# A graph-attention kernel: the two shares of a node's row weighted and added by one VectorE operation per head, with tanh in place of exp and the first three parts interleaved

## The reference

```python
N = 6250; E = 100000; IN_DIM = 256; HID = 64; HEADS = 4
h = (x @ W).reshape(n, HEADS, HID)            # x: normalised rows
e = leaky_relu(a_src[src] + a_dst[dst])       # src, dst: 206250 edges, then a self loop for each node
m = segment_max(e, dst);  num = exp(e - m[dst])
alpha = num / segment_sum(num, dst)[dst]
out = relu(segment_sum(alpha[:, :, None] * h[src], dst) + bias)
x = x + out
def step(h, _):                               # 30 times over layernorm(x)
    h = h + 0.01 * tanh(h)
    h = h * sigmoid(h)
    h = layernorm(h)
    return h @ W.T + b
x = x + (the rows after 30 steps)
```

## Time and profile before

| what | value |
|---|---|
| median of three runs | 4014.36 us (4007.2 to 4033.22) |
| the profiled execution | 4010.27 us, its span 4008.5 us |
| DVE busy | 3057.0 us (76% of the span) |
| POOL busy | 3000.3 us (75%) |
| ACT busy | 2421.6 us (60%) |
| PE busy | 1551.2 us (39%), nearly all of it after 2473 us |
| share of the chain that ended last on PE | 20%, of it the products 17% |

### The profile page before, as it was taken

One profiled execution on the slowest core, in us unless ns is written; L12 is line 12 of the kernel. 1 busy time (PEld: TensorE's weight loads), 2 busy tenths in 40 slices (PEclk: granted clock), 3 DMA queues, 4 the chain that ended last, 5 costly groups with the idle time before them and its releaser, 6 DMA issues.

```text
span 4008.5 us, 38964 instructions
## 1 busy us (share of the span) xinstructions
PE 1551.2 (39%) x7562; PEld 1329.0 (33%) x7562; DVE 3057.0 (76%) x7257; ACT 2421.6 (60%) x3681; POOL 3000.3 (75%) x2871
## 2 busy tenths in 40 slices
PE   3400000000000000000000001899999999999998
PEld 2300000000000000000000001788888888888887
DVE  7467585867768577685867766788988989888898
ACT  4334353534434344353534344689999999999997
POOL 7676676767676676766767672899999998889887
PEclk8755555555555555555555555999999999999999
DMA  7355565656555565565656563047777777777677
GB/s 201 113 177 193 182 207 181 213 174 214 195 190 201 169 223 178 190 209 168 225 164 218 189 198 126 23 117 179 189 185 185 181 177 177 173 177 175 177 183 193
DMA packets 649205, 720.45 MB, mean 180 GB/s; under 512 B 513249, under 2 KB 515458, under 8 KB 632948
## 3 DMA queue, kind: packets, MB, share of 16 engines
q1 hardware_dynamic: 563604, 486.62, 40.7%
q0 software_dynamic: 83824, 230.16, 20.0%
q10 hardware_dynamic: 1536, 1.18, 0.1%
HBM read 249.79 MB, written 352.38 MB: 150 GB/s over the span
## 4 chain that ended last, share of the span: by engine, by line
issue 25%; PE 20%; ACT 12%; DVE 12%; POOL 10%; DMA 9%; another core or an unknown queue 8%; SPq 2%; DVEq 0%; ACTq 0%; POOLq 0%
PE ps L1676 17%; ACT G L654 7%; POOL G L747 6%; DVE RS L983 5%; DMA turned<-hs 3%; DVE psum L964 3%; POOL h L1301 2%; PE ps L1662 2%; DMA h2T<-turned 2%; DMA sums<-G 2%; SPq L1231 1%; ACT hs L1398 1%; DMA G<-haug,idx 1%; ACT th L1409 1%
## 5 line engine op out<-in xcount | busy, mean ns | idle before, releaser
L747 POOL DMA_INDIRECT G<-haug,idx x1612 | 1526.6, 947 | 713.1 <-issue 481.8
L1676 PE MATMUL ps<-WT,h2T 128*128 128x256 f32 x5880 | 1338.8, 381 | 19.9 <-DMA h2T<-turned 18.8
L1676 PEld LDWEIGHTS ps<-WT,h2T 128*128 128x128 f32 x5880 | 1091.7, 191 | 175.8 <-DMA h2T<-turned 40.5
L983 DVE TENSOR_TENSOR_SCAN RS<-keep,psum 128x845 f32<-128x845 f32 x496 | 939.8, 1897 | 186.9 <-remote 109.9
L1301 POOL TENSOR_TENSOR h<-Hs,th 128x512 f32<-128x512 f32 (+1 forms) x750 | 937.8, 1262 | 129.9 <-ACT th L1409 124.6
L1068 PE MATMUL psum<-AD,ones 128*128 128x512 f32 x2 | 2.1, 1142 | 2284.9 <-DVE AD L1085 2284.9
L646 ACT ACTIVATE decay<-el,ZC 128x4 f32<-128x4 f32 x124 | 37.1, 299 | 1278.4 <-remote 568.0
L654 ACT ACTIVATE G<-RS 128x845 f32<-128x845 f32 x496 | 782.0, 1723 | 43.4 <-DVE RS L983 34.0
L1586 DVE SCALAR_TENSOR_TENSOR Hs<-ps,rs,b 128x256 f32<-128x256 f32 x1470 | 675.0, 459 | 145.3 <-PE ps L1676 132.6
L1068 PEld LDWEIGHTS psum<-AD,ones 128*128 128x128 f32 x2 | 0.5, 313 | 2285.2 <-DVE AD L1085 2285.2
L1568 DVE BATCH_NORM_STATS2 cst<-h 128x6 f32<-128x256 f32 x1470 | 546.3, 412 | 37.5 <-ACT h L1386 36.4
(11 more groups left out here) (164 smaller groups left out, 1196.9 us busy)
## 6 DMA issues: line engine op xcount, KB each, us to landing
sums<-G SPq DMA_DIRECT2D x124, 1716.0 KB
turned<-hs SPq DMA_DIRECT2D x444, 256.0 KB
G<-haug,idx POOLq DMA_INDIRECT x1612
h2T<-turned SPq DMA_TRANSPOSE x444
haug<-G SPq DMA_DIRECT2D x7, 924.0 KB
X<-x SPq DMA_DIRECT2D x7, 784.0 KB
out<-X SPq DMA_DIRECT2D x24, 224.0 KB
own<-haug SPq DMA_DIRECT2D x5, 924.0 KB, 5.5
```

Source lines behind the costliest of these rows:

```text
L747: pool.indirect_dma_start(out=G[:, u, t, :], out_offset=None, in_=haug[:, :], in_offset=bass.IndirectOffsetOnAxis(ap=idx[:, i % 2, u * T + ...
L983: v.tensor_tensor_scan(RS[:, k % 2, h, :, :].rearrange("p f t -> p (f t)"), keep[:, k % 2, :, :].rearrange("p f t -> p (f t)"), ps_m[:, h, ...
L1676: last = nc.tensor.matmul(ps_g[q.u][:, a * C:(a + 1) * C], h2T[:, q.u, (a * 2 + k) * P:(a * 2 + k + 1) * P], WT[:, k, :], start=(k == 0), ...
```

## The change

The PE products with the identity that joined the two rows go away, in all parts, with their PSUM buffers. In their place DVE's `joined` makes, for each tile and head, one scalar_tensor_tensor on 64 columns: gathered row times its weight plus the weighted own row, into `Hs`. `added` now reads this sum from `Hs` in SBUF instead of PSUM. The gathered rows' multiplication (`gathered`) goes away. The weights are made from tanh: with d = s - e, the shares 1 + tanh(d/2) and 1 + tanh(-d/2) stand in the same ratio as the two exps; the maximum is no longer taken, one operation adds the 1. ACT no longer calls exp after the attention stage; one tanh on a column is issued ahead. In parts 0 to 2 DVE's stages are interleaved (`all_spread` apart from `all_added`), ACT starts tanh after two rows instead of a whole part, POOL makes the roots of part 0 ahead of the last three fetches of part 2. The plans place a tile's join, sum and statistics at neighbouring steps; each part's rows are ready 3 or 4 steps earlier, and the table of passes shifts with it.

```diff
-PLANS = {FRONT: Plan(5, 1, 10, 17, 15, 16, 22, 23, 21, 3, 43, 48, 50, 1)}
+PLANS = {FRONT: Plan(5, 1, 10, 17, 15, 20, 18, 19, 3, 40, 45, 47, 1)}
 for b in range(FRONT + 1, NF):
     q = 24 + 80 * (b - FRONT - 1)
-    PLANS[b] = Plan(q, 8, q + 54, q + 62, q + 63, q + 64, q + 70, q + 72, q + 72, 11, q + 141, q + 148, q + 151, 3)
+    PLANS[b] = Plan(q, 8, q + 54, q + 62, q + 63, q + 69, q + 67, q + 68, 11, q + 137, q + 144, q + 147, 3)
...
             for b in range(FRONT):
                 for i in range(FT[b + 1] - FT[b]):
+                    if (b, i) == (FRONT - 1, 3):
+                        roots(0)
                     end_row(b, i)
...
-                nc.scalar.activation(share[:, b % 2, :, 0:n, :], below[:, b % 2, :, 0:n, :], ACT.Exp).then_inc(s_share, 1)
+                nc.scalar.activation(share[:, b % 2, :, 0:n, :], apart[:, b % 2, :, 0:n, :], ACT.Tanh, scale=0.5).then_inc(s_share, 1)
...
+            act.wait_ge(s_merged, 16)
+            nc.scalar.activation(spare[:, :], half_neg[:, 0:1], ACT.Tanh)
...
-                ch.add(v.tensor_tensor(nmax[:, i, 0:n, :], S[:, i, 0:n, SUMS:ROW], eself[:, t0:t1, :], ALU.max))
-                ch.wait()
-                v.tensor_tensor(below[:, i, 0, 0:n, :], S[:, i, 0:n, SUMS:ROW], nmax[:, i, 0:n, :], ALU.subtract)
-                v.tensor_tensor(below[:, i, 1, 0:n, :], eself[:, t0:t1, :], nmax[:, i, 0:n, :], ALU.subtract).then_inc(s_below, 1)
+                v.tensor_tensor(apart[:, i, 0, 0:n, :], S[:, i, 0:n, SUMS:ROW], eself[:, t0:t1, :], ALU.subtract)
+                v.tensor_tensor(apart[:, i, 1, 0:n, :], eself[:, t0:t1, :], S[:, i, 0:n, SUMS:ROW], ALU.subtract).then_inc(s_below, 1)
...
+                ch.add(v.tensor_scalar(share[:, i, :, 0:n, :], share[:, i, :, 0:n, :], 1.0, None, ALU.add))
+                ch.wait()
...
+            def joined(b, i):
+
+                for h in range(H):
+                    c = slice(h * HR, h * HR + HID)
+                    last = v.scalar_tensor_tensor(out=Hs[:, FT[b] + i, h * HID:(h + 1) * HID], in0=S[:, b % 2, i, c],
+                                                  scalar=part[:, b % 2, 0, i, h:h + 1], in1=own[:, b % 2, i, c],
+                                                  op0=ALU.mult, op1=ALU.add)
+                return last
...
-                ch.add(gathered(b, 0, n))
-                dve.wait_ge(s_own[b], 16)
-                own_rows(b, OWN_ACT[b], n).then_inc(s_scaled, 1)
+                dve.wait_ge(s_own[b % 2], 16 * (b // 2 + 1))
+                ch.add(own_rows(b, OWN_ACT[b], n))
+                ch.wait()
+                for i in range(OWN_ACT[b], n):
+                    joined(b, i)
+                dve.wait_ge(s_ownw, b + 1)
+                for i in range(OWN_ACT[b]):
+                    last = joined(b, i)
+                last.then_inc(s_scaled, 1)
...
-                if due(q, "scale"):
-                    b, i = due(q, "scale")
+                if due(q, "both"):
+                    b, i = due(q, "both")
+                    dve.wait_ge(s_joined, tiles_before(b) + i + 1)
+                    added(b, i, i + 1, Hs[:, FT[b] + i, :]).then_inc(s_taken, 1)
+                if due(q, "join"):
+                    b, i = due(q, "join")
                     if i == 0:
                         dve.wait_ge(s_part, b + 1)
-                    gathered(b, i, i + 1).then_inc(s_weighted, 1)
...
+                    dve.wait_ge(s_ownt, tiles_before(b) + i + 1)
+                    joined(b, i).then_inc(s_joined, 1)
...
-            for b in range(2):
-                shares(b)
-                norms(b)
-                all_weighted(b)
+            shares(0)
+            norms(0)
+            all_weighted(0)
+            shares(1)
             all_added(0)
+            norms(1)
+            all_spread(0)
+            all_weighted(1)
             all_added(1)
             shares(2)
+            all_spread(1)
             norms(2)
+            spread_of(At(0))
+            spread_of(At(1))
             all_weighted(2)
-            for q in range(4):
-                spread_of(At(q))
             all_added(2)
+            spread_of(At(2))
+            spread_of(At(3))
+            all_spread(2)
...
-            add_own(0)
-            add_own(1)
             transposes(At(0))
             transposes(At(1))
-            add_own(2)
...
-                if due(p, "add"):
-                    add_tile(*due(p, "add"))
```

More of the change, by code:

```diff
@@ L78, with __init__ @@
 class Plan:
-    def __init__(self, fetch, pace, below, share, norm, scale, own, add, both, step, mean, root, ready, every):
+    def __init__(self, fetch, pace, below, share, norm, own, join, both, step, mean, root, ready, every):
         n = QT
         self.at = dict(fetch=(fetch, pace, n), below=(below, 1, 1), share=(share, 1, 1), norm=(norm, 1, 1),
-                       scale=(scale, step, n), own=(own, step, n), add=(add, step, n), both=(both, step, n),
+                       own=(own, step, n), join=(join, step, n), both=(both, step, n),
                        spread=(both + 1, step, n), mean=(mean, 1, 1), root=(root, 1, 1), ready=(ready, every, n))
@@ L1180, in scan_ffn @@
         s_scaled = sem("s_scaled")
-        s_agg = sem("s_agg")
         s_added = sem("s_added")
```

90 lines of the change are left out of this document (28 added, 62 removed).

## The result

The changed kernel took 4027.45 us, the median of 12 runs (4021.8 to 4043.6), beside 4015.12 us for the kernel before, of 12 runs on the same chip (4001.63 to 4033.22). The ratio is 1.0048, with a 95% interval of 1.0031 to 1.0064 (the two medians alone stand at 1.0031): 12 to 26 us slower, where 20 us less was forecast. It lies inside the forecast range and within 1%, but on the other side of no change.

The account below looks back on a forecast made before the run. PE was taken as nearest bound, ACT right behind. Parts 4 to 7 (15), part 3 (1.5) and the front (4) sum to 20.5 us off 4010.3; with the median's 4.1 us that gives 3994 us, range 3974 to 4034.

Parts of the forecast that it names:

- PE's ceiling and ACT's loads: Parts 3 to 7: joins free PE of 30 us at most; ten ACT table loads go, 12.8 us.
- D: Rival: ACT holds the passes anyway, only 10.3 us of loads and 4 at the front count; 4000 us, chance 0.12.
- Parts 4 to 7, 15 us less: Window 2700 to 3350 us: PE loses 24.1 us, ACT 10.3, and the window shortens from 650 to 635 us.
- A head, 0.15 us: DVE's join: one operation on 64 columns takes 0.15 us, four heads of a tile 0.6 us.
- One wait for four heads, 0.5 us a tile: DVE's join: a tile's four heads go through on one wait for POOL, some 0.5 us.
- Rival A: Heads wait anew for POOL's `add`, roots let them pass; 0.8 us more per tile, 4011 us, chance 0.27.
- DVE idles 67 us, so this stays hidden: Parts 4 to 7: DVE's extra 19 us fit its idle time, busy 602 of 635 us; counted as nothing.
- Part 3, 1.5 us less: Passes 18 to 40: PE falls 0.86 us per tile, POOL does not; 1.5 us less, between 0 and 6.
- Ahead of the passes, 4 us less: Front: first tanh 5.5 us earlier, first silu only 1; 4 us less at the tanh of 2522.90, ends 1 and 5.5.
- Windows without parts that got slower, which none of this explains: Listed sign of being wrong: slower windows where no part is worked in; no size given.
- Rival B: One POOL operation between every two heads; 3.8 us more per tile, 4074 us, chance 0.09.
- C: Rival: PE's whole share comes through, ACT is no bound; 38 us less, 3976 us, chance 0.07.

Follow-up runs that it names:

- k1: Kernel before with tanh in place of exp, the maximum gone and one operation adding the 1, nothing else: ratio to before 0.9978.
- k19: The kernel of k1 again, on another chip: ratio to before 0.9994 (0.9976 to 1.0011).
- k14: Changed kernel's front and tanh, but parts 3 to 7 joined on PE with before's plans and table, part 0's roots behind the fetches: ratio to before 0.999.
- k17: k14 with parts 3 to 7 joined on DVE through PSUM instead of on PE: ratio to before 0.9968 (0.9934 to 1.0002).
- k18: The kernel of k17 again, unchanged, on the same chip as k19: ratio to before 0.9978 (0.996 to 0.9995).
- set 2: Runs on one other chip, with the kernel before and the changed kernel profiled once more: second stage 1534.2 and 1549.6 us.
- k4: Changed kernel, but joins of parts 3 to 7 read their second input from zeroed PSUM, own rows left out: second stage 1529.2 us.
- k11: Changed kernel with POOL's roots of part 0 behind the fetches again, nothing else: second stage 1547.8 us.
- k8: Changed kernel, tiles of parts 4 to 7 at a pitch of 12 steps instead of 11, joins at steps leaving 1 when divided by 3: second stage 1550.6 us.
- k9: Same edit as k8, but joins at steps that leave 2 when divided by 3: second stage 1549.9 us.

## Why the prediction was wrong, step by step

- **PE's ceiling and ACT's loads** were removed as read: no product with the identity is left, one table load instead of eleven. D gave the loads 10.3 us; tanh alone gained 8 (k1) and 2 (k19, with an interval that holds both).
- **Parts 4 to 7, 15 us less**: the first step that failed. It let PE's whole share count up to ACT's limit, since in the stretch without parts the fullest engine is busy 96 to 99%. The pairs k14/k17 and k19/k18 show 0 to 2 us for PE's 24. With PE relieved (k17) no engine is above 96.5%, and PE waits for turned rows instead. That the ring of all four engines and the transfers holds the passes is the likely reading; no run takes the transfers' share away.
- **A head, 0.15 us**: 0.195 us measured when POOL is quiet, so 0.8 and not 0.6 us a tile. The rows had no operation of this kind; a small miss.
- **One wait for four heads, 0.5 us a tile**: the second step that failed, and the larger one. Rival A's mechanism is what happens, tile by tile: an `add` blocks anew, a root mostly lets pass. The tile costs DVE (63.3 + 20.3)/28 = 2.99 us in set 2, against 24.7/28 + 0.41 = 1.30 before, so 1.7 us more; the forecast had 0.7 and A 1.5. A renewed wait was in the rows of before (the pair at 2550.83 in the earlier trace rows); I took the pair that spoke against it as equal evidence. It isn't: L1515 and L1516 (the means of part 4) read one SBUF tensor each, and L1516 started as POOL began a root.
- **"DVE idles 67 us, so this stays hidden"**: the third that failed, and A's own price with it. A added 22 us to DVE and let it fill 98% of the window, 645 us. Measured, 324 passes take 324 x 650/321 = 656 us, at a DVE busy 94.8% (the window moved by 13 us), and in set 2 324 x 650/323 = 652 us at 95.8%. So the passes slowed before DVE was full: the heads are one lump of up to 5 us, the moments behind it are late, and POOL's root with them. The rows of POOL's wait for `cmv`, 2.7 before and 20.5 us after, are this.
- **Part 3, 1.5 us less**: 5.5 us more (75.8 to 81.3, in both pairs). With heads that don't wait it is 73.2 (k4), 2.6 less. The step's gain was right, the same waits ate it.
- **Ahead of the passes, 4 us less**: 1.1 to 1.7 less up to affine 30, and 0.6 more at the tanh that the sum was made at. The first tanh gained 4.5, where the working had 5.5; the last fetch moved by 5.0 instead of 2.4 us. The roots are 2.9 of it (k11), the rest came with the wait for sixteen heads, which the working didn't have.
- **Windows without parts that got slower, which none of this explains**: they did, by 8.0 us over 800-1469 in the first pair and by 10.3 in set 2. From 1100 on it is the table of passes, which the plans shift by three or four steps; between 800 and 1100 the sets don't separate the tables. I had noted the shift as a fact of the change and given it no term.

In sum, in set 2: -1.1 at the front, +5.5 in part 3, +0.8 in parts 4 to 7 (+4.4 in the first pair), +3.1 and +7.2 behind them: 15.5 us. The forecast's -4, -1.5, -15 and 0 were each too favourable. That 4027 still lies in the range is no merit of the working: the range reached so far only for A's spread. Rival B's 3.8 us more a tile never came in the mean; C fell with PE's share, and D's 4000 is near k17's and k19's times, not this kernel's.

What stays open: why 33 us of DVE's time between k8 and k9 brought only 7 us up to affine 1100, and why the shifted table is worse at its end (about half of the loss lies between affines 1310 and 1340, 32.5 to 33.1 us against 29.3 to 31.3 with the table of before, where the chunks come in another order).

## What to carry to other kernels

An operation on VectorE that reads two SBUF tensors beside a busy GpSimd should be counted by the piece: every piece may wait anew for GpSimd's `add` or multiplication (0.7 us a tile with one piece here, 1.4 with four, 2.0 with eight). With one of the inputs in PSUM the wait was gone. In this ring of four engines at about 90% and more, PE relieved of 24 us gave back 0 to 2, and lumps of 2 to 5 us on DVE cost time although DVE was idle 5% of the window. And a plan that moves data's due time by a few steps moves the order of everything behind it, which had a price of its own here and can be tested alone.
